# Expert kernel with a residual: where the last experts run, when the residual is loaded, and which engine adds it

## The chip, the cores and the metric

The kernel runs on one core of a Trainium2 chip. The metric is the device time of one execution in microseconds. Three runs of the kernel before are shown; the profile is of a further execution.

## The reference, cut to what matters

Tokens: 4096 rows (4 x 1024) of 512 float32. An RWKV attention layer and a mixture-of-experts layer stand one behind the other, each between two layer norms and with a residual:

```python
x = x + _layernorm(_L0_attn_ref(_layernorm(x), ...))      # called x1 below
x = x + _layernorm(_L0_ffn_ref(_layernorm(x), ...))       # h = _layernorm(x1) goes in

# in the second line:
shared = _relu2(h @ shared_up_w.T) @ shared_down_w.T       # 1024 hidden
routed = _moe(h, idx, wts, w1, w2)                         # 64 experts, 6 a token,
                                                           # at most 128 tokens each, 256 hidden
return shared + routed
```

## The kernel before, in words

Work is in eight token tiles of 512 rows (NT = 8, ST = 4 blocks of 128 rows). The program of each engine is written out by hand, and semaphores tie them together; nothing is planned by a tool. There are three stages that matter.

**Attention** (to about 800 us) leaves x1 and h in DRAM. It isn't touched.

**The shared feed-forward and the experts.** The shared layer of a tile takes eight steps `j` (SJ = 8), each an `up` (12 matmuls, lines 578 to 580) and a `down` (12 matmuls, lines 595 to 597). Its result goes to the DRAM tensor `ysh`. Tiles 0 to 3 also do the routing. From step 6 of tile 4 on (FIRST_STEP), the experts are spread over the shared steps: `experts_until` (line 244) gives, for each of the 26 remaining steps, how many of the first E - ALONE = 56 experts must be done by its end. Every engine's program uses it. The last ALONE = 8 experts follow when the shared layer is through (lines 582, 701, 994).

An expert on the engines: POOL gathers its 128 tokens of h by an indirect DMA (line 1096, `gather`, four experts ahead); TensorE transposes them (610), multiplies by w1 (622) and, behind a relu (ACT, 938) and a square (DVE, 1528), by w2 (633); ACT scales by the gate (946); POOL adds the result into `ysh` by an indirect accumulating DMA (line 1116), the scatter. A scatter waits until the one before has landed (line 1114). Four buffers of each kind are used in turn, so that line 1518 (DVE) and line 945 (ACT) wait for the scatter of four experts earlier. SP loads w1 and w2 of four to five experts ahead (0.5 MB each, line 331).

In SP's loop over the experts, behind the last eight, the residual x1 is loaded in eight DMAs of 1 MB into the space of the shared layer's weights (lines 397 to 402), each behind a wait for TensorE's progress.

**The end.** When all 64 scatters have landed (`added`), SP loads `ysh` of tiles 0 to 3 (line 406). Tiles 4 to 7 hold the shared layer's result in SBUF still, and POOL adds the routed sums of `ysh` to it by four accumulating DMAs of 1 MB (line 1126). Then for each tile k in order: DVE takes the moments (`o_moments`, lines 1594 and 1597), POOL makes scale and offset from them (`o_scale`, four small operations, lines 1134 to 1139), ACT normalises in four blocks (line 1001), and x1 is added: blocks 0 and 1 on POOL (`o_add`, line 1146), blocks 2 and 3 on DVE (line 1604). Each engine's program has the additions of tile k-1 behind its work on the moments of tile k. SP stores the tile (line 410). All these SP transfers are 1 MB in rows of 2 KB.

Of the kernel before, what the change touches and what calls it, by code (L numbers as in the profile page):

```python
# [9 lines left out]
ALU = mybir.AluOpType  # L10
# [9 lines left out]
ST = TT // P  # L20
NT = N // TT
EPS = 1e-5
NEG_BIG = -1e38
E, GROUPS, TOPG, TOPK = 64, 8, 4, 6
# [4 lines left out]
SJ = SH // P  # L29
# [5 lines left out]
ROUTED = NT // 2  # L35
HALF = SJ // 2
FIRST_STEP = 6
ALONE = 8
KJ, VJ, RJ = range(3)
RING = 6  # L40
CEILING = 30.0
# [3 lines left out]
def sandwich(nc, t):  # L45

    ctx = ExitStack()
    with ctx:  # L48
# [15 lines left out]
        def sem(name):  # L64
            return ctx.enter_context(nc.semaphore(name))
# [54 lines left out]
        yout_ready ysh_stored logits_done score_ready sel_ready pos_ready placed route_step  # L120
        slots_ready scattered
        table_loaded gather_index scatter_index xd_turned xdT_ready e_up e_relu e_square e_down e_gated added
        out_stored ln4_stats ln4_moments ln4_rstd o_joined o_normed o_ready o_added""".split()
        names += [f"{n}{q}" for n, b in (("w1_loaded", WB), ("w2_loaded", WB), ("xd_loaded", EB)) for q in range(b)]
        names += [f"{n}{k}" for n in ("ysh_loaded", "x1_loaded") for k in range(NT)]
        S = {n: sem(n) for n in names}
# [86 lines left out]
        o_y = [rw[:, :, :], xres[:, :, :], hT, wkv[:, 0:ST * C].rearrange("p (s c) -> p s c", s=ST)] + [m[:, :, :] for m in youts[ROUTED:]]  # L213
        o_x = [weights[:, k, :].rearrange("p (s c) -> p s c", s=ST) for k in range(NT)]
        x_by_tile = t["x"].rearrange("(t s p) c -> t p s c", s=ST, p=P)
        x1_by_tile = t["x1"].rearrange("(t s p) c -> t p s c", s=ST, p=P)
# [27 lines left out]
        def experts_until(step):  # L244
            steps = SJ * (NT - ROUTED) - FIRST_STEP
            return max(0, min(steps, step + 1 - FIRST_STEP)) * (E - ALONE) // steps

# [11 lines left out]
        def shared_load(k):  # L259
            return 3 * k if k < ROUTED else 2 * ROUTED - 1 + k  # L260
# [24 lines left out]
        def _(sp):  # L285
# [38 lines left out]
            def load_h(k, number):  # L324

                sp.wait_ge(S["h_chunk_turned"], CK * number)
                sp.wait_ge(S["h_stored"], 16 * (k + 1))
                sp.dma_start(xin[:, :, :], h_by_tile[k]).then_inc(S["h_loaded"], 16)
# [55 lines left out]
            def expert(e):  # L384
                if within(e, WB + 1):
                    sp.wait_ge(S["e_up"], e + 2)
                    load_expert("w1", w1_sb, e + WB + 1)
                if within(e, WB):
                    sp.wait_ge(S["e_down"], e + 1)
                    load_expert("w2", w2_sb, e + WB)  # L390

            turned_before = {experts_until(SJ * (k - ROUTED) - 1) + 2: k + 1 for k in range(ROUTED + 1, NT - 1)}
            for e in range(E):
                expert(e)
                if e in turned_before:
                    load_h(turned_before[e], shared_load(turned_before[e]))
                k = e - (E - ALONE)
                if k >= 0:
                    sp.wait_ge(S["down_done"], SJ * NT)
                    sp.wait_ge(S["e_down"], e)  # L400
                    sp.wait_ge(S["x1_stored"], 16 * NT)
                    sp.dma_start(o_x[k], x1_by_tile[k]).then_inc(S[f"x1_loaded{k}"], 16)

            sp.wait_ge(S["added"], 16 * E)
            for k in range(ROUTED):
                sp.dma_start(o_y[k], ysh_by_tile[k]).then_inc(S[f"ysh_loaded{k}"], 16)
            for k in range(NT):
                sp.wait_ge(S["o_ready"], ST // 2 * (k + 1))
                sp.wait_ge(S["o_added"], ST // 2 * (k + 1))
                sp.dma_start(out_by_tile[k], o_y[k]).then_inc(S["out_stored"], 16)  # L410
            sp.wait_ge(S["out_stored"], 16 * NT)

# [2 lines left out]
        def _(pe):  # L415
# [220 lines left out]
            def expert(e):  # L636
                if e == 0:
                    pe.wait_ge(S["relu_ready"], SJ * ROUTED)
                    pe.wait_ge(S["placed"], NT)
                    pe.wait_ge(S["h_lo_ready"], CK * (ROUTED + 1))  # L640
                    for n in range(2):
                        xd_transpose(n)
                    e_first(0)
                if within(e, 2):
                    xd_transpose(e + 2)
                if within(e, 1):
                    e_first(e + 1)
                e_second(e)
# [50 lines left out]
            for k in range(NT):  # L699
                tile(k)  # L700
            for e in range(E - ALONE, E):
                expert(e)
# [3 lines left out]
        def _(act):  # L706
# [241 lines left out]
            def expert(e):  # L948
                if e == 0:
                    for n in range(2):  # L950
                        xdT_read(n)
                    e_relu(0)
                if within(e, 2):
                    xdT_read(e + 2)
                if within(e, 1):
                    e_relu(e + 1)
                e_gate(e)

            def tile(k):

                def next_hi(*chunks):
                    if j == SJ - 1 and has(k, 1):
                        for c in chunks:
                            h_hi(k + 1, c)

                for j in range(SJ):
                    r, i = 2 * k + j // HALF + 1, j % HALF
                    hidden(k, j)
                    if k < ROUTED:
                        if i == 1 and r < NT:  # L970
                            for c in range(CK):
                                h_copy((turn_bank, route_bank)[c % 2], r, c)
                        if i == 2 and r < NT:
                            scores(turn_bank, r)
                        if first(k) and j == 3:
                            ln3_normalise(NT - 1)
                        next_hi(*range(CK))
                    else:
                        todo = list(experts_in(k, j))
                        next_hi(0)  # L980
                        for e in todo[:1]:
                            expert(e)
                        next_hi(1)
                        for e in todo[1:2]:
                            expert(e)
                        next_hi(2)
                        for e in todo[2:]:
                            expert(e)
                        next_hi(3)
                yout_read(k)  # L990

            for k in range(NT):
                tile(k)
            for e in range(E - ALONE, E):
                expert(e)
# [10 lines left out]
        def _(pool):  # L1006
# [121 lines left out]
            def o_scale(k):  # L1128
                w = o_slot(k)
                pool.wait_ge(S["ln4_moments"], ST * (k + 1))  # L1130
                if k >= 2:
                    pool.wait_ge(S["o_normed"], ST * (k - 1))
                pool.sem_inc(S["pool_step"], 1)  # L1133
                pool.tensor_scalar(rstd[:, w, :], mv[:, w, :, 1], EPS, None, ALU.add).then_inc(S["ln4_rstd"], 1)  # L1134
                pool.tensor_scalar(offset[:, w, :], mv[:, w, :, 0], -1.0, None, ALU.mult).then_inc(S["ln4_rstd"], 1)  # L1135
                pool.wait_ge(S["ln4_rstd"], 4 * k + 2)
                pool.tensor_tensor(rstd[:, w, :], rstd[:, w, :], neg_half[:, :], ALU.pow).then_inc(S["ln4_rstd"], 1)  # L1137
                pool.wait_ge(S["ln4_rstd"], 4 * k + 3)
                pool.tensor_tensor(offset[:, w, :], offset[:, w, :], rstd[:, w, :], ALU.mult).then_inc(S["ln4_rstd"], 1)  # L1139

            def o_add(k):

                pool.wait_ge(S[f"x1_loaded{k}"], 16)
                for s in range(ST // 2):
                    pool.wait_ge(S["o_normed"], ST * k + s + 1)  # L1145
                    pool.tensor_tensor(o_y[k][:, s, :], o_y[k][:, s, :], o_x[k][:, s, :], ALU.add).then_inc(S["o_ready"], 1)  # L1146

            for k in range(NT):
                o_scale(k)
                if k >= 1:  # L1150
                    o_add(k - 1)
            o_add(NT - 1)


        @block.vector
        def _(dve):
# [373 lines left out]
            def expert(e):  # L1530
                if e == 0:
                    index_scatter(0)
                    e_square(0)
                if within(e, 1):
                    e_square(e + 1)
                    index_scatter(e + 1)
                if within(e, EB):
                    index_gather(e + EB)
# [41 lines left out]
            for k in range(NT):  # L1580
                tile(k)
            for e in range(E - ALONE, E):
                expert(e)
# [15 lines left out]
            def o_add(k):  # L1599

                dve.wait_ge(S[f"x1_loaded{k}"], 16)
                for s in range(ST // 2, ST):
                    dve.wait_ge(S["o_normed"], ST * k + s + 1)
                    dve.tensor_tensor(o_y[k][:, s, :], o_y[k][:, s, :], o_x[k][:, s, :], ALU.add).then_inc(S["o_added"], 1)

            for k in range(NT):
                o_moments(k)
                if k >= 1:
                    o_add(k - 1)
            o_add(NT - 1)  # L1610


# [33 lines left out]
```

## Time and profile before

| | us |
|---|---|
| median of 3 runs | 1543.37 |
| lowest and highest run | 1539.24, 1548.29 |
| profiled execution, its time | 1531.26 |
| profiled execution, its span | 1529.5 |
| busy in the span: PE | 1206.2 (79%) |
| busy: DVE, ACT, POOL | 822.8, 591.0, 487.5 |
| first scatter starts | 997.5 |
| last scatter starts | 1458.7 |

The 1.8 us between the span and the time of the profiled execution lie around the program. "Share" of the DMA is the mean busy share of its 16 engines. PE is the matmul, PEld the weight load on TensorE; SPq is the queue of SP. A name such as `v_sb<-ysh` is destination and source of an instruction.

### The profile page before, as it was taken

Reading aid. Unit: us, or ns where it says so; the run is one execution under the profiler, and the core shown is the slowest. Engines: PE = TensorE matmul, PEld = TensorE weight load, DVE = VectorE, ACT = ScalarE, POOL = GpSimd, SP = SyncE. Lnnn points to the kernel's source line nnn. Section 1 sums busy time; section 2 is a strip of 40 time slices with the busy share of each in tenths; the row PEclk is TensorE's granted clock in tenths of the full one; section 3 lists DMA queues with packets and bytes.
Section 4 is the critical chain, followed back from the end, with each engine's and each line's share of the span. In section 5 each row is a group of like instructions: output and inputs, shape, how many; then the busy total and the mean of one; then the engine's idle time right before and its main releaser. Section 6 shows DMA issues by size and latency. Waiting matters only on the chain. (4 is left out here: it accounts for less than half of the span.)

```text
span 1529.5 us, 15480 instructions
## 1 busy us (share of the span) xinstructions
PE 1206.2 (79%) x4832; PEld 793.2 (52%) x4832; DVE 822.8 (54%) x1964; ACT 591.0 (39%) x993; POOL 487.5 (32%) x470
## 2 busy tenths in 40 slices
PE   6989999888989578748677486899998999997500
PEld 3434444333444247547566374677676777775400
DVE  4789889787989897637475373222122122120025
ACT  3456665555666645122121111233333233332114
POOL 1001110110110023745626557123333332433247
PEclk9999999999999779778887697999999999998755
DMA  7201023030203306111101202169978787989787
GB/s 294 83 3 52 28 83 104 7 110 28 82 1 138 110 28 248 50 62 28 56 28 30 81 1 83 43 171 273 239 207 250 218 221 202 242 235 267 230 197 255
DMA packets 82863, 193.82 MB, mean 127 GB/s; under 512 B 12000, under 2 KB 12384, under 8 KB 81760
## 3 DMA queue, kind: packets, MB, share of 16 engines
q1 hardware_dynamic: 60192, 154.98, 29.9%
q0 software_dynamic: 22592, 37.90, 12.6%
q8 instruction: 36, 0.59, 0.2%
q14 instruction: 43, 0.35, 0.1%
HBM read 141.80 MB, written 51.12 MB: 126 GB/s over the span
## 5 line engine op out<-in xcount | busy, mean ns | idle before, releaser
L461 PE MATMUL bank<-mix_ring,weights 128*128 128x512 f32 x768 | 349.9, 614 | 22.7 <-ACT bank L776 13.5
L461 PEld LDWEIGHTS bank<-mix_ring,weights 128*128 128x128 f32 x768 | 149.4, 197 | 212.3 <-issue 206.3
L1083 POOL DMA_INDIRECT slots<-xnd x192 | 200.6, 1045 | 162.1 <-DVE xnd L1402 89.4
L1116 POOL DMA_INDIRECT ysh<-k_sb,mixf x64 | 101.3, 1582 | 236.7 <-DMA ysh<-k_sb,mixf 148.5
L1503 DVE TENSOR_TENSOR k_sb<-k_sb 128x512 f32<-128x512 f32 x64 | 47.9, 749 | 212.0 <-ACT k_sb L905 178.3
L1528 DVE TENSOR_TENSOR run_max<-run_max 128x256 f32<-128x256 f32 x64 | 27.2, 425 | 247.0 <-ACT run_max L938 236.9
L905 ACT ACTIVATE k_sb<-bank 128x512 f32<-128x512 f32 x64 | 38.2, 597 | 264.8 <-PE bank L580 136.1
L468 PE MATMUL bank<-weights,rw 128*128 128x512 f32 x256 | 118.0, 616 | 19.6 <-DVE rw L1266 9.9
L1020 POOL TENSOR_SCALAR rstd<-mv 128x4 f32<-128x4 f32 x16 | 10.6, 664 | 365.6 <-DVE mv L1179 347.4
L578 PE MATMUL bank<-h_high,ffn_w 128*128 128x512 f32 x256 | 114.1, 446 | 12.8 <-issue 6.7
L595 PE MATMUL bank<-ffn_w,s_split 128*128 128x512 f32 x256 | 116.9, 457 | 2.5 <-issue 2.5
L420 PE MATMUL bank<-ident,xin 128*128 128x128 f32 x240 | 40.7, 317 | 91.8 <-ACT xnT L801 68.6
L596 PE MATMUL bank<-ffn_w,s_split 128*128 128x512 f32 x256 | 105.1, 411 | 0.0
L597 PE MATMUL bank<-ffn_w,s_split 128*128 128x512 f32 x256 | 104.8, 410 | 0.1
L580 PE MATMUL bank<-h_high,ffn_w 128*128 128x512 f32 x256 | 102.7, 401 | 0.0
L579 PE MATMUL bank<-h_low,ffn_w 128*128 128x512 f32 x256 | 102.6, 401 | 0.0
L622 PE MATMUL bank<-xnT,wkv 128*128 128x128 f32 x768 | 100.8, 288 | 0.1
L622 PEld LDWEIGHTS bank<-xnT,wkv 128*128 128x128 f32 x768 | 96.6, 204 | 0.3 <-issue 0.3
L1096 POOL DMA_INDIRECT xres<-h,mixf x64 | 63.4, 991 | 100.2 <-DVE mixf L1513 79.0
L468 PEld LDWEIGHTS bank<-weights,rw 128*128 128x128 f32 x256 | 50.5, 199 | 84.6 <-issue 64.2
L633 PE MATMUL bank<-wkv,run_max 128*128 128x512 f32 x192 | 91.8, 601 | 0.0
L420 PEld LDWEIGHTS bank<-ident,xin 128*128 128x128 f32 x240 | 33.7, 164 | 101.9 <-ACT xnT L801 69.8
(197 smaller groups left out, 2171.2 us busy)
## 6 DMA issues: line engine op xcount, KB each, us to landing
wkv<-in_w SPq DMA_DIRECT2D x96, 512.0 KB
state<-in_w SPq DMA_DIRECT2D x32, 512.0 KB
xin<-h SPq DMA_DIRECT2D x15, 1024.0 KB
xin<-in_x SPq DMA_DIRECT2D x8, 1024.0 KB, 5.4
xres<-in_x SPq DMA_DIRECT2D x8, 1024.0 KB, 5.2
x<-xres SPq DMA_DIRECT2D x8, 1024.0 KB
weights<-x SPq DMA_DIRECT2D x8, 1024.0 KB, 8.9
h<-hb SPq DMA_DIRECT2D x7, 1024.0 KB, 4.5
```

What stands on the lines that cost most here:

```text
L461: mm = pe.matmul(bank[:, d, :], W(j)[:, ck, d * P:(d + 1) * P], mix_slot(4 * j + ck), start=(ck == 0), stop=(ck == CK - 1))
L468: mm = pe.matmul(bank[:, s, :], rw[:, ck, s * P:(s + 1) * P], W(3)[:, ck, :], start=(ck == 0), stop=(ck == CK - 1))
L578: pe.matmul(bank, hi, hT_hi[:, ck, :], start=(ck == 0), stop=False)
L579: pe.matmul(bank, hi, hT_lo[:, ck, :], start=False, stop=False)
L580: mm = pe.matmul(bank, lo, hT_hi[:, ck, :], start=False, stop=(ck == CK - 1))
L595: pe.matmul(y_bank[:, s, :], hi, sd[0][:, j, :], start=(j == 0), stop=False)
L596: pe.matmul(y_bank[:, s, :], hi, sd[1][:, j, :], start=False, stop=False)
L597: mm = pe.matmul(y_bank[:, s, :], lo, sd[0][:, j, :], start=False, stop=(j == SJ - 1))
L622: mm = pe.matmul(e_up_bank[:, i * CAP:(i + 1) * CAP], w1_sb[e % WB][:, ck, i * P:(i + 1) * P], xdT[q][:, ck, :], start=(ck == 0), stop=(ck ...
L633: mm = pe.matmul(route_bank, e_act[b][:, i, :], w2_sb[e % WB][:, i, :], start=(i == 0), stop=(i == IK - 1))
L1083: pool.indirect_dma_start(t["slots"], bass.IndirectOffsetOnAxis(ap=slot[:, s, c:c + 1], axis=0), choice[:, s, c, :], None, bounds_check=E ...
L1116: pool.indirect_dma_start(t["ysh"], bass.IndirectOffsetOnAxis(ap=scatter_token[:, q:q + 1], axis=0), e_out[q], None, compute_op=ALU.add).t ...
```

## The change

The number of experts alone at the end goes from 8 to 2, so that 62 instead of 56 are spread over the same 26 shared steps. SP no longer loads x1 in the loop over the experts: x1 of tile 0 is loaded when the shared layer is through, those of tiles 1 to 4 behind the `ysh` load of the tile before each, and those of tiles 5 to 7 behind these. All four additions of a tile are on DVE, and POOL's additions and their semaphore are gone. SP's store waits for DVE's semaphore alone.

```diff
-ALONE = 8
+ALONE = 2
@@ SP, behind expert(e) and load_h in the loop over the experts
-                k = e - (E - ALONE)
-                if k >= 0:
-                    sp.wait_ge(S["down_done"], SJ * NT)
-                    sp.wait_ge(S["e_down"], e)
-                    sp.wait_ge(S["x1_stored"], 16 * NT)
-                    sp.dma_start(o_x[k], x1_by_tile[k]).then_inc(S[f"x1_loaded{k}"], 16)
-
+
+            sp.wait_ge(S["down_done"], SJ * NT)
+            sp.wait_ge(S["x1_stored"], 16 * NT)
+
+            def load_x1(k):
+                sp.dma_start(o_x[k], x1_by_tile[k]).then_inc(S[f"x1_loaded{k}"], 16)
+
+            load_x1(0)
             sp.wait_ge(S["added"], 16 * E)
             for k in range(ROUTED):
                 sp.dma_start(o_y[k], ysh_by_tile[k]).then_inc(S[f"ysh_loaded{k}"], 16)
+                load_x1(k + 1)
+            for k in range(ROUTED + 1, NT):
+                load_x1(k)
             for k in range(NT):
-                sp.wait_ge(S["o_ready"], ST // 2 * (k + 1))
-                sp.wait_ge(S["o_added"], ST // 2 * (k + 1))
+                sp.wait_ge(S["o_added"], ST * (k + 1))
                 sp.dma_start(out_by_tile[k], o_y[k]).then_inc(S["out_stored"], 16)
@@ POOL
-            def o_add(k):
-
-                pool.wait_ge(S[f"x1_loaded{k}"], 16)
-                for s in range(ST // 2):
-                    pool.wait_ge(S["o_normed"], ST * k + s + 1)
-                    pool.tensor_tensor(o_y[k][:, s, :], o_y[k][:, s, :], o_x[k][:, s, :], ALU.add).then_inc(S["o_ready"], 1)
-
             for k in range(NT):
                 o_scale(k)
-                if k >= 1:
-                    o_add(k - 1)
-            o_add(NT - 1)
@@ DVE, o_add
-                for s in range(ST // 2, ST):
+                for s in range(ST):
```

## Rows read from the trace of the kernel before

**Rows 1.** Windows: stretch and length; busy us (count) by engine; PEclk, DMA share, GB/s.
```profile
1200.00:1392.00 192.00, 186.47 (x1004) 144.38 (x1003) 35.76 (x136) 64.76 (x118) 69.43 (x55) 0.99 0.85 227
1392.00:1463.40 71.40, 36.06 (x155) 25.50 (x153) 4.09 (x25) 12.00 (x23) 18.63 (x14) 0.75 0.79 224
1463.40:1529.50 66.10, 0.00 (x0) 0.00 (x0) 33.66 (x80) 23.42 (x32) 43.82 (x52) 0.50 0.89 254
```

**Rows 2.** Timeline of PE, a late interleaved expert: start us, us, instruction.
```profile
1356.76 0.60 PE L610 MATMUL bank<-ident,xres 128*128 128x128 f32 x4
...
1360.30 0.79 PE L595 MATMUL bank<-ffn_w,s_split 128*128 128x512 f32 x1
...
1363.46 0.60 PE L610 MATMUL bank<-ident,xres 128*128 128x128 f32 x4
```

**Rows 3.** The scatter's line: for what POOL waited before it, us, times.
```profile
  DMA ysh<-k_sb,mixf: 148.5, 34
```

**Rows 4.** Waits of PE from 990 to 1392 us: total, times, longest.
```profile
PE bank L610 <- DMA xres<-h,mixf: 12.1, 9, 3.7
```

**Rows 5.** Timeline of POOL, scatters: start, us, [idle before <-releaser].
```profile
1041.73 1.57 POOL L1116 DMA_INDIRECT ysh<-k_sb,mixf  x1 [4.12 <-DMA ysh<-k_sb,mixf]
...
1389.79 1.58 POOL L1116 DMA_INDIRECT ysh<-k_sb,mixf  x1 [5.17 <-issue]
1395.63 1.57 POOL L1116 DMA_INDIRECT ysh<-k_sb,mixf  x1 [2.99 <-ACT k_sb L946]
...
1447.36 1.55 POOL L1116 DMA_INDIRECT ysh<-k_sb,mixf  x1 [6.61 <-DMA ysh<-k_sb,mixf]
...
1458.71 1.55 POOL L1116 DMA_INDIRECT ysh<-k_sb,mixf  x1 [3.97 <-DMA ysh<-k_sb,mixf]
```

**Rows 6.** DMA issues: queue, count, KB, us from issue to landing.
```profile
weights<-in_Wk SPq DMA_DIRECT2D x1, 1024.0 KB, 7.5
weights<-in_Wo SPq DMA_DIRECT2D x1, 1024.0 KB, 12.6
xin<-ysh POOLq DMA_DIRECT2D x1, 1024.0 KB, 36.5
out<-rw SPq DMA_DIRECT2D x1, 1024.0 KB, 16.1
out<-xin SPq DMA_DIRECT2D x1, 1024.0 KB, 4.2
```

**Rows 7.** Timeline of SP's queue: start us, us, instruction.
```profile
1.31 0.49 SPq L288 DMA_DIRECT2D weights<-in_Wk  x1
...
3.71 0.45 SPq L288 DMA_DIRECT2D weights<-in_Wo  x1
...
1484.66 0.38 SPq L410 DMA_DIRECT2D out<-rw  x1
```

**Rows 8.** Timeline of DVE in the last stretch.
```profile
1472.30 0.38 DVE L1597 BATCH_NORM_AGGREGATE mv<-stats 128x2 f32<-128x6 f32 x4
...
1492.79 2.48 DVE L1594 BATCH_NORM_STATS2 stats<-wkv 128x6 f32<-128x512 f32 x4 [4.10 <-DMA wkv<-ysh]
...
1495.60 1.26 DVE L1604 TENSOR_TENSOR xnT<-xnT,weights 128x512 f32<-128x512 f32 x2
1496.77 2.46 DVE L1594 BATCH_NORM_STATS2 stats<-v_sb 128x6 f32<-128x512 f32 x4
```

**Rows 9.** Timeline of POOL in the last stretch.
```profile
1466.04 3.02 POOL L1126 DMA_DIRECT2D xin<-ysh  x1
...
1472.90 0.24 POOL L1134 TENSOR_SCALAR rstd<-mv 128x4 f32<-128x4 f32 x1 [3.84 <-DVE mv L1597]
...
1506.03 0.62 POOL L1134 TENSOR_SCALAR rstd<-mv 128x4 f32<-128x4 f32 x1
...
1508.63 2.49 POOL L1146 TENSOR_TENSOR v_sb<-v_sb,weights 128x512 f32<-128x512 f32 x2
```

**Rows 10.** Timeline of ACT, the normalisation of tile 0.
```profile
1474.89 2.93 ACT L1001 ACTIVATE rw<-rw,offset,rstd 128x512 f32<-128x512 f32 x4 [28.40 <-POOL offset L1139]
```

More of the change, by code:

```diff
@@ L122, in sandwich @@
         table_loaded gather_index scatter_index xd_turned xdT_ready e_up e_relu e_square e_down e_gated added
-        out_stored ln4_stats ln4_moments ln4_rstd o_joined o_normed o_ready o_added""".split()
+        out_stored ln4_stats ln4_moments ln4_rstd o_joined o_normed o_added""".split()
         names += [f"{n}{q}" for n, b in (("w1_loaded", WB), ("w2_loaded", WB), ("xd_loaded", EB)) for q in range(b)]
```

## Prediction

> **What bounds the kernel now.** I read the windows first, then TensorE's timeline, then the waits, then the end engine by engine; everything up to the first scatter stays as it is. In the interleaved stretch PE is busy 186.5 of 192 us and the DMA engines 0.85 of the time; once the experts are alone PE falls to 36 of 71.4 us, while the DMA share stays at 0.79; in the last 66.1 us PE does nothing and the DMA share is 0.89 [rows 1]. An interleaved expert takes PE 3.54 us (1356.76 to 1360.30) and a half step of the shared layer 3.16, 6.70 together [rows 2]. That looks like a TensorE stage, but a second chain runs nearly as slowly: 34 of 64 scatters waited for the one before to land [rows 3], and nine times PE waited for a gather, which POOL issues just ahead of a scatter [rows 4]. From the sixth scatter (1041.73) to the one at 1389.79 there are 49 cycles, 7.10 us each [rows 5]. The nine cycles from there to the last scatter, beside eight x1 loads, take 7.66; the last two, beside little, 11.35 together [rows 5]. The last scatter needs 4.7 us more, to 1463.4. So two bounds of about 7 us an expert lie on each other in the expert stage. The end then starts with eight loads: the fourth SP load lands at 1492.79, 29.4 us in [rows 8], POOL's last at 1466.04 + 36.5 = 1502.5, 39.1 us in [rows 6, 9]; after this POOL paces the tiles, with 2.60 us of scale and offset and 2.49 of additions for each [rows 9].
>
> **The change, part by part.** The sum is made against the profiled execution, span 1529.5 and time 1531.26, which is 12.1 us under the median of the three runs; I carry the difference over to the median.
>
> *Six more experts among the shared steps.* PE's 26 steps get 6 x 3.54 = 21.2 us longer. If PE alone counted, the scatter that followed PE's last interleaved expert at 1395.63 [rows 5] would move to 1416.9, two experts later than it 11.35, and the landing at 1432.9: 30.5 us sooner than 1463.4. The scatter chain doesn't allow that if its cycle keeps to what it was. Expert 61, the last interleaved, is 56 cycles behind the sixth scatter. The trace has no row of an expert stage at this density, so the cycle is bounded by 6.7 (the pace of [rows 2], which the chain kept up with in late tiles) and 7.66. The nearest is 7.10 at almost the same DMA load; its average contains pauses at tile boundaries in which the shared layer kept PE from experts, and a chain that lags behind has work in store there. I take 7.0. That puts scatter 61 at 1041.7 + 392 = 1433.7, the last at 1445.1, landed at 1449.8: **13.6 us gained**.
>
> *x1 loads out of the expert stage.* Eight plain DMAs go, and SP's waits on `e_down` with them; nothing in SP's queue is behind these but weight loads that have four buffers of lead. Their price was the difference of 7.66 to 7.10 over nine cycles, 5 us, and it is inside the gain above. x1 of tile 0 is now issued when the shared layer is through, some 25 us ahead of `added`; behind it SP has only that wait. Cover: the last scatters. Without it, 2.5 us (next paragraph); taken at zero.
>
> *Seven x1 loads at the end.* Here the change pays. SP's queue becomes y0, x1 of 1, y1, x1 of 2, y2, x1 of 3, y3, x1 of 4 to 7, eleven MB, while POOL's four accumulating loads run. The store of tile 0 shows how such a queue is served: issued at 1484.66, it landed 16.1 us later, at 1500.8, 8.0 us behind the last y load at 1492.79 [rows 6 to 8]. So transfers of SP go in order, at 8.0 us a MB while POOL's accumulates last. The fifth MB, now y2, lands at 37.4 us ; the accumulates end at 39.1. Plain loads alone went faster: Wk at 1.31 + 7.5 = 8.8, Wo, three MB later, at 3.71 + 12.6 = 16.3, 2.5 us each [rows 6, 7]. So x1 of 3 lands at 41.1, y3 at 43.6, the last x1 at 53.6. Before, y3 was there at 29.4; DVE takes the moments in tile order and stands still before it, although POOL's tiles 4 to 7 are there. From y3 on, DVE sets the pace.
>
> *Additions.* POOL loses 16 additions, 2.49 us a tile. DVE gains 16: two took 1.17 us from start to start (1495.60 to 1496.77), the moments 2.81 (1492.79 to 1495.60) [rows 8], so 2.81 + 2.34 = 5.15 us a tile on DVE in place of 5.09 on POOL. Nothing is won in pace, the bound only changes engine. The moments of tile 7 start at 43.6 + 4 x 5.15 = 64.2 and end at 67.0. Then 2.2 us to the normalisation (1472.68 to 1474.89 [rows 8, 10]), 2.93 for it, 0.6 for the last addition, 0.4 to the issue and 4.2 for the store [rows 6]: 77.3. POOL's small operations beside DVE additions grow: 0.62 against 0.24 us for the first of four [rows 9]; I add 0.8, to 78.1. **The end loses 12.0 us.**
>
> No row prices stores that queue behind one another. The stores of tiles 0 to 4 queue up behind the last x1, at 53.6. At 2.5 us (the plain load) all eight are over by 73.6 and hidden; at 4.2 (a store alone [rows 6]) they are over at 87.2, 9 us more. A lone store's 4.2 contains its latency, so I take the nearer, the queued load, and keep 9 for the range.
>
> Sum: -13.6 + 12.0 = -1.6, so 1541.8 from the median.
>
> **Two rules.** The trace shows the x1 loads hidden under the experts before, at about 5 us [rows 5], and the row of the end says what the queue charges there. The Trainium skill, "DMA: Bandwidth & Descriptors", Rules for kernel authors, says to issue a DMA early and wait late so that its cost overlaps compute; it speaks against this change. By the rule alone the end would lose seven loads of 2.5 us, 17.5, and the sum would be +3.9; by the rows, where only three x1 loads stand ahead of y3, it is -1.6.
>
> The trace shows POOL's first small operation at 0.62 us instead of 0.24 beside DVE's additions [rows 9], a slowdown and no full stop. The Trainium skill, "SBUF — State Buffer", section SBUF: two separate sides, says a DVE operation with two SBUF inputs and a GpSimd operation that reads SBUF exclude each other for the whole instruction. By it POOL's scale for tile 7 could stand behind all four additions of tile 6, 2.3 us instead of my 0.8: sum -0.1. By the row: -1.6.
>
> **The rivals.**
> A, the forecast: the chain keeps 6.8 to 7.15 us, 1531 to 1550. For it: at 7.0 us an expert the DMA load is that of before.
> B, TensorE sets the stage: the chain follows PE, -30.5 + 12.0 = -18.5, 1525. For it: PE at 97% and scatters at PE's pace late in the stage. Against it: the waits of [rows 3, 4], and steps with three experts, now ten instead of four, which ask for 3.54 + 6.32/3 = 5.65 us each, less than the 5.7 of the last two cycles, beside which little ran.
> C, the slower one: the scatter's cycle itself grows when weights, gathers and scatters are packed closer. Its place is POOL's wait before line 1116, behind which the gather four ahead is queued, so PE starves too. At 7.33, halfway from 7.00 to the 7.66 that nine cycles had under extra loads, the last scatter lands at 1468.3: +4.9 + 12.0 = +16.9, 1560. It turns the sign over 0.5% from a cycle of 7.17. For it: a DMA share of 0.85 leaves little. Against it: a chain that is slow spreads its own load.
> D, the x1 loads at the end are hidden anyway: were SP's ring served more often than 8.0 us a MB beside POOL's accumulates, y3 could land near 29 again, and the end would be 0.5 longer than before (stores, four additions): -13.1, 1530. For it: the loads and the accumulates are different queues. Against it: the 8.0 held for loads and for a store.
> That the change doesn't do what it says can't be: counts and additions are in the code.
>
> **How the numbers follow.** 0.5% is 7.7 us, about what a measurement can tell. A 0.55 (0.10 faster, 0.40 same, 0.05 slower), B 0.14 (faster), C 0.21 (slower), D 0.10 (0.09 faster, 0.01 same). Together 0.33, 0.41, 0.26. The likeliest case gives 1541.8. The range goes down to B's value, 1525, and up to nearly C's, 1558; the store queue's 9 us on top of A (1551) are inside. What is left out is the half of B under its value and a good half of C.
>
> **What would show it.** In the changed profile: the scatter to 61 in cycles of 7.0, so that `added` comes at about 1450 (B: 1433, C: 1468); no `L402` beside the last experts; the wait of DVE's moments for `wkv<-ysh` ending 43.6 us into the end, against 29.4; additions on POOL gone and DVE's tile pace at 5.15; out<-rw landing over 25 us behind its issue; the end 78 us long. It is wrong if y3 lands before 35 us (then D), if PE has few waits for gathers and the cycle is under 6.8 (B), or if the cycle is over 7.17 (C); if the stores follow each other at over 3 us, the end is longer than 80.

## The result, and the profile after

The changed kernel takes 1548.84 us in the median of 12 runs, the kernel before 1540.33 in the 12 runs made for it: a ratio of 1.0074, 95% interval 1.0043 to 1.0105. It is slower by 11 us at the middle of the interval and by 7 at its lower end. In a later comparison of the same two kernels the ratio was 1.0013 (0.9975 to 1.0052), which can't be told from 1. The profiles are sharper than the times, because they allow the stages to be compared without the routing ahead of them: the first scatter starts anywhere from 997 to 1020 us in executions of kernels whose programs are the same up to there (a faster chip, told of at the end, apart). From the first scatter to the end of the span the kernel before needs 532.1 us and the changed one 539.2 (538.1 when profiled again). So by the profiles the change costs 6 to 7 us, some 0.45%. The forecast was -1.6 us, "no change". The measured median lies within the stated range, 1525 to 1558 us; it is the direction that was missed.

The windows of the changed kernel, columns as in [rows 1]; the stretches are the middle of the interleaved stage, what follows it, and the end:

```profile
1203.30:1395.30 192.00, 178.14 (x948) 135.39 (x947) 35.75 (x136) 63.25 (x114) 70.06 (x54) 0.98 0.84 223
1439.00:1461.04 22.04, 9.47 (x39) 5.67 (x37) 1.08 (x6) 4.41 (x8) 6.39 (x4) 0.85 0.51 96
1461.04:1540.00 78.96, 0.00 (x0) 0.00 (x0) 41.82 (x96) 23.41 (x32) 24.56 (x36) 0.50 0.99 306
```

Against [rows 1] there are two differences. With more experts packed in, TensorE is busy *less* of the same 192 us, 178 instead of 186, and the DMA engines carry 223 instead of 227 GB/s. And the end is 12.9 us longer, with a DMA share of 0.99.

TensorE's wait for gathers, from 993 to 1437 us, answers to [rows 4]; the scatter's line to [rows 3]; POOL's timeline to [rows 5], with the first, sixth and last three scatters:

```profile
PE bank L613 <- DMA xres<-h,mixf: 31.2, 20, 5.5
```

```profile
  DMA ysh<-k_sb,mixf: 141.8, 33
```

```profile
1000.74 1.62 POOL L1119 DMA_INDIRECT ysh<-k_sb,mixf  x1 [0.46 <-issue]
...
1045.16 1.57 POOL L1119 DMA_INDIRECT ysh<-k_sb,mixf  x1 [4.34 <-DMA ysh<-k_sb,mixf]
...
1444.90 1.55 POOL L1119 DMA_INDIRECT ysh<-k_sb,mixf  x1 [4.04 <-DMA ysh<-k_sb,mixf]
1450.80 1.55 POOL L1119 DMA_INDIRECT ysh<-k_sb,mixf  x1 [4.36 <-ACT k_sb L949]
1456.28 1.55 POOL L1119 DMA_INDIRECT ysh<-k_sb,mixf  x1 [3.93 <-DMA ysh<-k_sb,mixf]
```

From the sixth scatter to that of expert 61 it is 399.7 us for 56 cycles, 7.14 each. PE's waits for gathers in the interleaved stretch went from 12.1 us (9 times) to 31.2 (20 times).

The end, in SP's queue and on DVE:

```profile
1461.07 0.38 SPq L407 DMA_DIRECT2D rw<-ysh  x1
...
1463.36 7.53 SPq L407 DMA_DIRECT2D xnT<-ysh  x1
1470.93 7.71 SPq L402 DMA_DIRECT2D weights<-x  x1
1478.68 7.72 SPq L407 DMA_DIRECT2D wkv<-ysh  x1
1486.45 17.89 SPq L402 DMA_DIRECT2D weights<-x  x4
1504.38 2.65 SPq L413 DMA_DIRECT2D out<-rw  x1
```

```profile
1482.36 2.47 DVE L1587 BATCH_NORM_STATS2 stats<-xres 128x6 f32<-128x512 f32 x4 [12.14 <-DMA xres<-ysh]
...
1498.39 2.47 DVE L1587 BATCH_NORM_STATS2 stats<-xnT 128x6 f32<-128x512 f32 x4 [10.77 <-DMA xnT<-ysh]
...
1505.07 2.47 DVE L1587 BATCH_NORM_STATS2 stats<-wkv 128x6 f32<-128x512 f32 x4 [1.41 <-DMA wkv<-ysh]
...
1510.26 2.46 DVE L1587 BATCH_NORM_STATS2 stats<-v_sb 128x6 f32<-128x512 f32 x4
```

y3 (`wkv`) lands 44.0 us into the end (1505.07 - 1461.04), against 29.4 before [rows 8]. While POOL's accumulates run, SP's queue is full, and each further issue takes 7.5 to 7.7 us of SP's time: the pace of one MB. From y3 on DVE takes 5.18 us a tile.

### The profile page after: what moved, and what is told of

The parts are those of the page before. It is cut to its first block and busy times, and to the rows that moved or that the text cites. A ratio compares the mean times of both kernels' runs of the same rounds, so it can differ in the third digit from the quotient of the medians.

```text
span 1540.0 us, 15457 instructions
## 1 busy us (share of the span) xinstructions
PE 1201.5 (78%) x4832; PEld 785.2 (51%) x4832; DVE 831.1 (54%) x1980; ACT 591.9 (38%) x993; POOL 468.6 (30%) x454
## 5 line engine op out<-in xcount | busy, mean ns | idle before, releaser
L581 PE MATMUL bank<-h_high,ffn_w 128*128 128x512 f32 x256 | 115.8, 452 | 9.9 <-ACT k_sb L908 9.9
L598 PE MATMUL bank<-ffn_w,s_split 128*128 128x512 f32 x256 | 114.7, 448 | 0.0
L599 PE MATMUL bank<-ffn_w,s_split 128*128 128x512 f32 x256 | 103.6, 405 | 2.4 <-issue 2.4
L600 PE MATMUL bank<-ffn_w,s_split 128*128 128x512 f32 x256 | 103.8, 406 | 1.3 <-issue 1.2
L583 PE MATMUL bank<-h_high,ffn_w 128*128 128x512 f32 x256 | 104.1, 407 | 0.0
```

Source lines behind the costliest of these rows:

```text
L581: pe.matmul(bank, hi, hT_hi[:, ck, :], start=(ck == 0), stop=False)
L583: mm = pe.matmul(bank, lo, hT_hi[:, ck, :], start=False, stop=(ck == CK - 1))
L598: pe.matmul(y_bank[:, s, :], hi, sd[0][:, j, :], start=(j == 0), stop=False)
L599: pe.matmul(y_bank[:, s, :], hi, sd[1][:, j, :], start=False, stop=False)
L600: mm = pe.matmul(y_bank[:, s, :], lo, sd[0][:, j, :], start=False, stop=(j == SJ - 1))
```

## The experiments

One measure serves all: the stage, from the start of the first scatter to SP's first `ysh` load, and the end, from there to the end of the span. Both repeat within 1 us where the kernel is the same (460.3 and 459.4; 78.9 and 78.7). Where only the other part of the kernel was edited, a stage repeats within 1.2 us, also between chips (before 466.0, adds_only 467.2; changed 460.3, sums_first 460.2, plain_sums 460.6). A kernel with "one run" leaves part of the work out, so that it has one time and no ratio.

| kernel | stage us | end us | sum | ratio to before, 95% |
|---|---|---|---|---|
| before | 466.0 | 66.1 | 532.1 | 1 |
| changed | 460.3 | 78.9 | 539.2 | 1.0074 (1.0043, 1.0105) |
| changed_again | 459.4 | 78.7 | 538.1 | 1.0013 (0.9975, 1.0052) |
| adds_only | 467.2 | 64.5 | 531.7 | 0.9978 (0.9949, 1.0006) |
| eight_alone | 455.8 | 78.7 | 534.5 | 1.0005 (0.9977, 1.0032) |
| x1_ahead | 471.2 | 64.2 | 535.4 | 1.0003 (0.9975, 1.0031) |
| sums_first | 460.2 | 75.3 | 535.5 | 1.0024 (1.0002, 1.0045) |
| index_first | 463.6 | 78.7 | 542.3 | 1.0015 (0.9980, 1.0050) |
| two_targets | 420.1 | 78.9 | 499.0 | one run |
| two_targets_eight | 428.5 | 78.8 | 507.3 | one run |
| half_weights | 431.2 | 78.8 | 510.0 | one run |
| plain_sums | 460.6 | 66.5 | 527.1 | 0.9964 (0.9926, 1.0003) |
| plain_eight | 454.8 | 66.3 | 521.1 | 0.9923 (0.9895, 0.9951) |

**The additions by themselves** (adds_only: the kernel before, o_add only on DVE).

```diff
-                for s in range(ST // 2, ST):      # DVE
+                for s in range(ST):
-                if k >= 1:                        # POOL
-                    o_add(k - 1)
-            o_add(NT - 1)
```

> The kernel before with all additions on DVE and none on POOL, nothing else changed. Theory 1: the tile pace at the end stays 5.15 us on DVE in place of 5.17 on POOL; end stage 66 to 67 us, ratio 1.000 within 0.002. Rival (DVE as the bound costs more): end of 68 us or more.

The end is 64.5 us, 1.6 less than before, though the tile pace is the same. The gain is at the last tile. Before, ACT began its normalisation at 1519.06 and the last addition on DVE was over at 1523.75, on POOL at 1524.87, where two additions took 3.45 us. Now DVE does the four in 2.74 us, one behind each block of ACT:

```profile
1439.50 2.46 DVE L1593 TENSOR_TENSOR sr<-sr,weights 128x512 f32<-128x512 f32 x4
1443.49 2.74 DVE L1593 TENSOR_TENSOR xin<-xin,weights 128x512 f32<-128x512 f32 x4 [1.52 <-ACT xin L1000]
```

This part of the change is harmless. By the profile it is slightly good; the times, 0.9949 to 1.0006, can't tell.

**The packing undone** (eight_alone: the changed kernel with the old count).

```diff
-ALONE = 2
+ALONE = 8
```

> The changed kernel with eight experts alone again instead of two. Theory 1 (the six experts put among the shared steps saved nothing, since TensorE waited for gathers there): alone and without x1 loads beside them an expert costs 5.8 us, so that the time from first scatter to last landing is 398 + 8 x 5.8 + 4.7, about 450 us, 10 us less than in the changed kernel; the end stays 79 us; ratio to before about 1.001. Rival (packing the experts closer did help, by the 5.7 us seen): 460 to 466 us and no faster than the changed kernel. PE's waits for gathers in the interleaved stretch: Theory 1 some 12 us in 9 waits, as before, against 31 in 20 of the changed kernel.

The stage is 4.5 us *shorter* than with two alone, 455.8 against 460.3. PE's waits for gathers in the interleaved stretch are those of before again:

```profile
PE bank L613 <- DMA xres<-h,mixf: 12.0, 15, 1.8
```

An expert alone costs 51.4 / 8 = 6.4 us, more than the 5.8 expected; six experts more among the shared steps stretch these from 399.6 us (first to 56th scatter) to 444.2 (to the 62nd), 7.4 us an expert, although they are 3.54 us of work for PE [rows 2]. So the packing loses, and the two parts of the expert stage oppose each other: with x1 gone 467.2 falls to 455.8 (adds_only to eight_alone, 11.4), and the packing gives 4.5 of this back. These 4.5 us are between two chips; on one chip they are 4.4 (sums_first against eight_alone) and 5.8 (plain_sums against plain_eight). The longer stretch adds up as 21.2 us of matmuls (6 x 3.54), 19.2 us more of waits for gathers, and some 4 us that are not accounted for.

**x1 loads ahead of the last landing** (x1_ahead).

```diff
-            load_x1(0)
+            for k in range(NT):
+                load_x1(k)
             sp.wait_ge(S["added"], 16 * E)
...
-                load_x1(k + 1)
-            for k in range(ROUTED + 1, NT):
-                load_x1(k)
```

> The changed kernel, but all eight x1 loads are issued when the shared layer is through, ahead of the wait for the last scatter. Theory 1 (the end is slower because y3 stands behind three x1 loads at 8 us a MB): the end stage, 79.0 us in the changed kernel, goes back to 66 to 67 us, and the last two or three scatter cycles grow from 5.8 to some 7 to 9 us, so 460 us from the first scatter to the landing of the last become 463 to 467: 7 to 10 us faster than the changed kernel, ratio to the kernel before about 1.000 to 1.003. Rival (the end is slow for another reason, DVE's additions or the stores): the end stays over 75 us.

The end goes to 64.2 us, so it was the x1 loads in it that made it long. But the stage grows by 11 us. The last scatter cycles and the last landing show it (with POOL's first accumulate at their end):

```profile
1364.13 1.55 POOL L1117 DMA_INDIRECT ysh<-k_sb,mixf  x1 [4.12 <-DMA ysh<-k_sb,mixf]
1373.39 1.54 POOL L1117 DMA_INDIRECT ysh<-k_sb,mixf  x1 [7.72 <-DMA ysh<-k_sb,mixf]
1381.79 1.55 POOL L1117 DMA_INDIRECT ysh<-k_sb,mixf  x1 [6.85 <-DMA ysh<-k_sb,mixf]
1389.74 1.41 POOL L1127 DMA_DIRECT2D v_sb<-ysh  x1 [6.41 <-DMA ysh<-k_sb,mixf]
```

9.3, 8.4 and 7.7 us where eight_alone and the changed kernel have 5.5 to 5.9 and 4.8. My 463 to 467 was too low: a scatter beside queued plain loads takes half as long again, and (this is argued, not tried) with two experts alone there is no long stretch over which to spread eight of them.

**The sums first** (sums_first).

```diff
             for k in range(ROUTED):
                 sp.dma_start(o_y[k], ysh_by_tile[k]).then_inc(S[f"ysh_loaded{k}"], 16)
-                load_x1(k + 1)
-            for k in range(ROUTED + 1, NT):
+            for k in range(1, NT):
                 load_x1(k)
```

> The changed kernel with the four ysh loads on SP ahead of the x1 loads of tiles 1 to 7. Theory 1: y3 lands at 29.4 us of the end as in the kernel before, the first x1 behind it at 37.4; DVE stands at the addition of tile 1 until then and has 36.3 us left after that: end of 73.7 us instead of 79.0, 5 us faster than the changed kernel. Rival (the end is bound by the total of bytes or by the stores): 78 us or more.

75.3 us, 3.6 under the changed kernel where 5.3 were expected. y3 is there early (27.6 us from issue to landing) but the wait has moved to x1 of tile 1:

```profile
1414.48 2.50 DVE L1596 TENSOR_TENSOR xres<-xres,weights 128x512 f32<-128x512 f32 x4 [13.14 <-DMA weights<-x]
1416.89 2.47 DVE L1586 BATCH_NORM_STATS2 stats<-wkv 128x6 f32<-128x512 f32 x4
```

The fifth MB of SP lands 37.2 us into the end (1414.48 - 1377.32), as y2 did in the changed kernel (1498.39 - 1461.04 = 37.3), whichever tensor it holds.

The DMA engines say why no order of the loads helps much more. These are the ends of sums_first and of plain_sums (below), columns as in [rows 1]:

```profile
1377.32:1452.60 75.28, 0.00 (x0) 0.00 (x0) 41.86 (x96) 23.42 (x32) 23.74 (x36) 0.50 1.03 320
1480.63:1547.10 66.47, 0.00 (x0) 0.00 (x0) 49.50 (x104) 23.42 (x32) 30.45 (x40) 0.50 0.98 363
```

Share times length is the time that the DMA engines were busy, an estimate, as a share can read over 1. Before it is 0.89 x 66.1 = 59 us; in the changed kernel, 0.99 x 78.96 = 78; in sums_first the engines never rest. Seven MB more are 19 us of DMA work, and the end before had only 7 us in which the engines were free. That leaves 12 of the 12.8 us by which the end grew. The order of the loads is worth the 3.6 us of sums_first and, with the engines always busy there, little more.

**The accumulates taken away** (plain_sums: `routed` are four free pieces of SBUF; POOL adds blocks 0 and 1, DVE blocks 2 and 3, ahead of the moments).

```diff
-            for k in range(ROUTED, NT):                                # POOL
-                pool.dma_start(o_y[k], ysh_by_tile[k], accum_op=ALU.add)...
+            for k in range(NT):                                        # SP
+                sp.dma_start(o_y[k] if k < ROUTED else routed[k - ROUTED], ysh_by_tile[k])...
+                if k + 1 < NT:
+                    load_x1(k + 1)
...
+                        dve.tensor_tensor(o_y[k][:, s, :], o_y[k][:, s, :], routed[k - ROUTED][:, s, :], ALU.add)...
```

> The changed kernel with the four accumulating loads of POOL replaced by plain loads of ysh into free SBUF on SP's queue (order y0, x1 of 1, y1, x1 of 2 and so on), and the routed sums of tiles 4 to 7 added by POOL (two blocks) and DVE (two blocks). Theory A (the x1 loads were dear only because each MB on SP's ring waits for a MB of an accumulating load on POOL's): y3 lands near 22 us instead of 44, SP's loads follow each other at 2.5 to 2.6 us, and the end takes 16 loads and 8 stores at that pace, 64 to 68 us in place of 78.7, although its bytes are the same. Theory B (the end is bound by the bytes it moves): y3 no earlier than 35 us, end 75 us or more. Expert stage 460 us as in the changed kernel.

Fifteen loads and eight stores, the same payload as in the changed kernel's end, take 66.5 us instead of 78.9, and y3 lands at 22.5 us. SP's issues now follow each other at about 2.6 us, for loads and for stores:

```profile
1485.82 2.44 SPq L404 DMA_DIRECT2D weights<-x  x1
1488.30 2.55 SPq L409 DMA_DIRECT2D wkv<-ysh  x1
1490.89 2.58 SPq L404 DMA_DIRECT2D weights<-x  x1
1493.52 2.58 SPq L409 DMA_DIRECT2D wkv<-ysh  x1
...
1513.01 2.58 SPq L414 DMA_DIRECT2D out<-rw  x1
1515.63 2.59 SPq L414 DMA_DIRECT2D out<-xres  x1
```

Theory B, a bound by bytes, falls. A bound by the time of the DMA engines doesn't: they are busy for 0.98 x 66.5 = 65 us here and for 78 in the changed kernel, so the four loads cost 13 us of DMA time more as accumulates than as plain loads, about 3 us a MB. The seven x1 loads, 18 us at 2.6 each, are inside the 65; what they cost by themselves beside plain loads was not measured. Nor is it told apart whether the accumulation or POOL's queue makes the four dear, because the edit changes both.

**The same with eight alone** (plain_eight: `ALONE = 8` in plain_sums).

> The same as plain_sums with eight experts alone. From eight_alone (456 us from first scatter to the ysh loads) and an end of 64 to 68: 520 to 524 us in place of the 532 of the kernel before, ratio 0.992 to 0.995. If theory B of plain_sums holds, ratio 1.000 or more.

521.1 us, ratio 0.9923 (0.9895 to 0.9951): faster than the kernel before, and by its stages than the changed one (521.1 against 539.2). It takes from the change the additions and the late x1 loads, leaves the packing, and has the plain loads of plain_sums.

**The chain of scatters broken** (two_targets; odd experts add into a second tensor `ysh2`).

```diff
-                    pool.wait_ge(S["added"], 16 * e)
+                    pool.wait_ge(S[f"added{e % 2}"], 16 * (e // 2))
...
-                pool.indirect_dma_start(t["ysh"], ...
+                pool.indirect_dma_start(t[("ysh", "ysh2")[e % 2]], ...
```

> The changed kernel with the odd experts' results added into a second DRAM tensor, so that a scatter waits for the one two before it and not for the last; same bytes, same number of DMAs. The odd experts' results are left out of the sum, and the second tensor is zeroed at the start. Theory Q: POOL no longer stands before each scatter, gathers are issued sooner, the interleaved stretch falls from 444 us to 425 to 435 us (PE's work alone is 409), PE's waits for gathers to under 18 us. Theory L: within 3 us of 444, since the bytes are the same.

The stage falls by 40 us, to 420.1; first to 62nd scatter takes 406.2 us, below my 425 to 435. PE's wait for gathers is nearly gone:

```profile
PE bank L617 <- DMA xres<-h,mixf: 4.7, 4, 1.9
```

and POOL waits for no landing any more:

```profile
1394.25 0.98 POOL L1103 DMA_INDIRECT xres<-h,mixf  x1 [3.71 <-DVE mixf L1511]
1395.64 1.57 POOL L1123 DMA_INDIRECT ysh<-k_sb,mixf  x1 [0.41 <-issue]
1400.93 0.98 POOL L1103 DMA_INDIRECT xres<-h,mixf  x1 [3.72 <-DVE mixf L1511]
1402.31 1.58 POOL L1123 DMA_INDIRECT ysh<-k_sb,mixf  x1 [0.41 <-issue]
```

With the same bytes, theory L (gathers are late whenever they are issued, because of load) falls as the main cause. "PE's work alone is 409" was wrong too: from the first to the 62nd scatter PE was busy 405.5 us in the changed kernel and 394.1 here, at a granted clock of 0.98 there and 0.99 here (21 fewer matmuls are on record here, which is some 4 of the 11 us).

**The same with eight alone** (two_targets_eight).

> two_targets with eight experts alone instead of two; again odd experts' results are left out of the sum. It tells what the packing of experts is worth once the chain of scatters is broken. Theory Q (the chain was what kept the packing from paying): TensorE is the bound of both, an expert alone costs TensorE's own latencies of 5 us or more against the 3.5 it adds among the shared steps, so the stage from first scatter to ysh loads is 8 to 14 us longer than the 420.1 of two_targets. Rival (packing never pays, since experts run as fast alone): within 3 us of 420.

428.5 us, 8.4 more than with two alone. First to 56th scatter is 383.4 us, so the six packed experts cost (406.2 - 383.4) / 6 = 3.8 us each, close to their 3.54 us on PE. Once the chain is broken the packing pays what the change wants from it; with the chain, the same edit loses 4.5 us.

**Fewer bytes** (half_weights).

```diff
+                half = CK * HID // 2 if e >= WB else CK * HID
-                sp.dma_start(dst[e % WB]..., t[name][e])
+                sp.dma_start(dst[e % WB]...[:, 0:half], t[name][e][:, 0:half])
```

> The changed kernel with only half of each expert's w1 and w2 loaded from the fifth expert on (the other half stays that of an earlier expert), 0.5 MB less an expert, a third of its bytes. Theory L: gathers and scatters land sooner, PE's waits for gathers fall from 31 us to under 10, and the interleaved stretch to about 420 us. Theory Q: scatter cycles get somewhat shorter, but the order on DVE keeps most of the waits: stretch 432 us or more.

The stretch is 414.0 us and PE waits 6.9 us for gathers, as theory L had it and not theory Q. A scatter that POOL had to wait for came 6.4 us behind the last one (29 cycles), against 7.2 in the changed kernel (33). So the length of the chain's link depends on what else the DMA engines carry. This and two_targets belong together: the chain is what holds the stage, and load is what makes its link long. Neither theory is right alone.

**The index ahead of the square** (index_first).

```diff
+                if within(e, EB):
+                    index_gather(e + EB)
                 if within(e, 1):
                     e_square(e + 1)
                     index_scatter(e + 1)
-                if within(e, EB):
-                    index_gather(e + EB)
```

> The changed kernel with DVE writing the index of the gather for expert e+4 ahead of the square of expert e+1 instead of behind it. Theory Q (queue order: a gather is issued late because its index stands on DVE behind a square that waits for TensorE's next expert, and on POOL behind a scatter that waits for a landing): the first half of this goes, PE's waits for gathers in the interleaved stretch fall from 31 us to 20 or less, and the stretch from 444 to 430 to 436 us. Theory L (load: gathers land late because the DMA engines are busy, whenever they are issued): waits and stretch within 3 us of the changed kernel.

A miss for theory Q as I had put it. The wait for gathers stays at 30.5 us, the stretch is 446.8:

```profile
PE bank L613 <- DMA xres<-h,mixf: 30.5, 18, 5.9
```

DVE's place of the index isn't the reason; what is left is POOL's queue, in which each gather stands behind a scatter that waits for a landing, and two_targets shows that it is this wait.

**The changed kernel again.**

> The changed kernel itself, beside the others on the same chip. Expected from its first profile: interleaved stretch (first to 62nd scatter) 444 us, PE waiting for gathers some 31 us there, 460 us from first scatter to the ysh loads, end 79 us; ratio to the kernel before 1.004 to 1.010. No theory is at stake but that the stages repeat within 2 us.

The stages repeat (443.2, 29.6 us of waits, 459.4, 78.7). The ratio of the times, 1.0013, is below the 1.004 to 1.010 that were expected; its interval reaches into them.

## Why the prediction was wrong

*The end: right.* 78.1 us were worked out and 78.9 measured; y3 at 43.6, measured 44.0; the last x1 ahead of the stores; stores 2.5 us apart (measured 2.5: out<-rw landed at 1504.38 + 13.9 = 1518.3 and out<-xres at 1507.08 + 13.7 = 1520.8), so hidden; DVE's pace 5.15, measured 5.18. The rows that carried it, one store that landed 8.0 us behind the load ahead of it and the loads at the kernel's start, held. The sum followed the order of the loads and didn't look at the DMA engines' time. That time, 59 us before and seven times 2.6 for the x1 loads, is 77 us and would have given nearly the same end; sums_first shows that it binds, since with y3 early the end still took 75.3. One sign was wrong: out<-rw landed 14 us behind its issue and not over 25, because the full queue held SP's issue itself back. POOL's small operations beside the additions were the 0.8 us long that I added, or a little more (the third took 1.33 us in place of 1.04); all four took 2.73 us beside additions (1508.18 to 1510.91) and 1.96 without (1470.43 to 1472.39). They did not stand behind all four additions. The Trainium skill ("SBUF — State Buffer", SBUF: two separate sides) describes an exclusion for the whole of one instruction; the stop for the whole run of additions was my reading of it, and the trace does not show that one.

*The additions: right in pace, wrong by 1.6 us at the last tile,* where POOL's slow additions had been on the path (adds_only). In the sum for the end this made no difference, since I had worked out the new tail from ACT's and DVE's rows.

*The x1 loads out of the stage: undersized.* I priced them at 5 us, the difference of 7.66 to 7.10 us a cycle over nine cycles, and said that this was inside the 13.6. Measured with nothing else changed it is 11.4 us (adds_only 467.2, eight_alone 455.8): the nearest row for a scatter cycle among experts alone was not the 7.10 of the packed stage, but the last two cycles, 5.7 us.

*Six more experts among the shared steps: the step that failed.* I took 7.0 us for the scatter's cycle, on the ground that "a chain that lags behind has work in store" at the tile boundaries. It was 7.14 (7.09 in changed_again), and 56 x 0.14 = 7.8 us is all that was missing from the gain (5.8 us from the sixth scatter to the last landing instead of 13.6). The store doesn't exist. A late scatter holds up the gather behind it in POOL's queue, and TensorE, which needs that gather two experts later, comes to wait too: 31 us instead of 12. At a boundary the chain then finds no finished expert. Here ACT finishes the last expert ahead of a boundary of the changed kernel, the scatter follows 0.8 us later, and the next expert is finished 13 us on (rows of ACT's and POOL's timelines in order of time):

```profile
1300.34 0.69 ACT L949 ACTIVATE k_sb<-bank,mixf 128x512 f32<-128x512 f32 x1 [1.34 <-PE bank L636]
1301.87 1.57 POOL L1119 DMA_INDIRECT ysh<-k_sb,mixf  x1 [0.40 <-issue]
1313.41 0.69 ACT L949 ACTIVATE k_sb<-bank,mixf 128x512 f32<-128x512 f32 x1 [1.33 <-PE bank L636]
1314.94 1.58 POOL L1119 DMA_INDIRECT ysh<-k_sb,mixf  x1 [0.40 <-issue]
```

The pauses between scatters there are 10 to 13 us in the changed kernel, 9 to 13 before. Instead of two bounds at 6.7 and 7.0 us of which the larger counts, they feed each other. two_targets shows it: with the link cut, TensorE's waits go and the six experts cost what they cost TensorE. The weighing by which I set rival B aside (its waits and the dense steps) was right, but the same waits spoke for a price nearer to 7.1 or above, and the forecast took a value below the nearest row from an argument that no row supported.

Behind the 13.6 stood two shares, 5 for the x1 loads and so 8.6 for the packing. Measured, the x1 loads gave 11.4 and the packing took 4.5. The two errors, 6.4 and 13.1 us, cancel for the most part; that the sum for the stage missed by no more than 8 us is luck.

*The rivals.* C named the place, POOL's wait before line 1116 with the gather queued behind, and that PE would starve; its size, 7.33, was too large, and 7.14 lies just under the 7.17 from which it was to decide. D is excluded by the 44.0 us. Both losses together, not one, make the 6 to 7 us: against the kernel before, additions -0.4, x1 loads to the end +2.8 (-11.4 in the stage, +14.2 in the end), packing +4.7. Each of these differences is uncertain by about 1 us.

*The rule of the skill.* The Trainium skill, "DMA: Bandwidth & Descriptors", Rules for kernel authors, says to issue early and wait late, so that the fixed setup cost overlaps compute. It spoke against the change, and the sum by it was +3.9. The sign was right: issued early beside the scatter chain the eight loads cost 11.4 us, at the end beside accumulates seven of them 14.2. But early was not free here, because what ran beside the loads was a chain of DMA latencies. With plain loads in place of the accumulates an end with the seven x1 loads is as long as the end before without them (66.5 and 66.1 us).

## What to carry to other kernels

Before more work is put under a stage that looks bound by TensorE, look for a chain of waits through one queue (here scatter, landing, next scatter, with the gathers behind them): if its cycle is already as long as the engine's, the new work costs a cycle of the chain, 7.4 us here for 3.5 us of matmuls, and alone it would have been cheaper (6.4). Before transfers are moved into another stage, work out how long the DMA engines are free there: 7 us were free at this end, and 19 us of work came in. A plain transfer queued beside the accumulating DMAs of POOL went at 8 us a MB here, and beside plain ones at 2.6. When two bounds lie within a few per cent of each other and each can hold up the other, the larger of the two is a floor and not the forecast.

## What the runs showed of the hardware that was not expected

The four kernels adds_only, eight_alone, x1_ahead and sums_first ran on a chip where the first scatter started at 917 to 920 us, and all others on chips where it started at 997 to 1021; the kernel before itself took 1455.3 us in the median there and 1540 to 1556 elsewhere. The attention is over at 600 us, and not at about 800 as the text ahead of the prediction says: SP issues the last store of x1 at 600.62 in the kernel before. The routing's first indirect DMA starts at 605 us there and at 612 in x1_ahead, so the attention isn't shorter on that chip, and the stages from the first scatter on are those of the table. The time lies in the routing stretch, from 590 to 1020 us. On the slower chips ACT and DVE stand still there for up to 20 us at a time, with a releaser that the profile calls "remote", 212.8 us in 32 waits over both engines in the kernel before; its longest group:

```profile
ACT k_sb L905 <- remote: 124.5, 13, 18.3
```

In the four profiles of the faster chip there is no such wait. What they are was not tried and stays open; they also vary from one execution to the next (166.6 to 232.1 us in nine profiles). Their sum alone doesn't order the starts of the experts: the kernel before, with 212.8 us, has its first scatter at 997.5, and half_weights, with 166.6, at 1010.5. So why the times of one kernel spread by 2% while its later stages repeat within 1 us stays open too.

While accumulates run, a DMA share of 1.03 stands for 254 GB/s (1461.04 to 1498.39 us of the changed kernel); from 1505 us on, with plain loads and stores, the changed kernel moves 349 GB/s at a share of 0.92. A high share tells which kind of transfer is in the way only together with the bytes.
